# Node update of a graph network: the 35 tiles behind attention in 7 batches of 5 in place of 5 batches of 7

## The chip, the cores and the metric

One core of one Trainium2 chip runs the whole kernel. The metric is the device time of one execution in microseconds (us). Before the change it is 3775.62 us, the median of 3 runs (3770.89 to 3781.33).

## What is computed

The kernel is one attention layer and four graph convolutions over a graph of 6250 nodes with 128 features and 200000 edges. The change touches the part between them, which is done for every node alone once attention has summed its messages:

```python
agg = jax.ops.segment_sum(ft_s * a[:, :, None], dst, num_segments=n)   # 10 heads of 13
out = jax.nn.elu(agg)
out = out.reshape(n, H * DH) @ hr_w + hr_b
out = out + h_skip                       # the normalized input
out = _layer_norm(out, in_w, in_b)
skip2 = out
out = jax.nn.elu(out @ w1 + b1)          # 128 -> 512
out = jax.nn.elu(out @ w2 + b2)          # 512 -> 128
return out + skip2
...
x = x + _L0_gnn_ref(...)
h = jnp.maximum(_layernorm(x, axis=-1), 0.0)   # input of the convolutions
```

All of it is in fp32.

## The kernel before

The 6250 nodes are 49 tiles of 128 nodes. The program is a row of stages with a barrier of all engines between them: `prelude`, `attention`, `node_update`, `general_attention`, `node_update` once more (`redo`), `convolutions`. `general_attention` and the second update are behind a flag that is set only for irregular graphs; they have no rows in the trace. `attention` itself updates the first 14 tiles (FT = 2 * 7) while it runs. `node_update` takes the other 35, in MANY = 5 batches of BATCH = 7 tiles (BW = 896 nodes).

A batch i goes through these steps, with the names of the functions in the code:

- `divide` (DVE) divides the sums by the softmax denominators, `exp_attention` (ACT) and `elu_attention` (DVE) form the first ELU.
- `turn_attention` (PE) transposes the tiles into `el_ps`, `attention_turned` (ACT) copies them to `elT` and `el3T`.
- `project` (PE) is for each tile three matmuls into `el_ps`: the normalized input `hnT` against the identity, `elT` against `hr_w`, and `el3T` (the last columns and the bias) against `hr_3`. The `hnT` of the batch is loaded from DRAM into one of two buffers.
- `first_stats`, `coefficients` (DVE), `deviation`, `normal` (ACT), `second_norm` (DVE) are the layer norm; the result is `s2`, and x takes it up as well.
- `turn_second` (PE), `second_turned` (ACT copy to `s2T`).
- `quarter` 0 to 3 (PE) is the product with w1, one 128-wide part of the 512 each; `exp_quarter` (ACT) and `elu_quarter` (DVE) are its ELU, to `uT`.
- `down` (PE), in two halves a, is the product with w2; `exp_out` (ACT) and `elu_out` (DVE) give `vT`; `turn_out` (PE) transposes it back; `add_feed_forward` (DVE) adds it to x.
- `stats`, `coefficients`, `deviation`, `rectified`, `turn_h`, `hT_out` are the next layer norm and its transpose to `hT`.

The order of the work on each engine is written out by hand as a software pipeline. In cycle i PE does the transposes and quarters of batch i, the projection of batch i + 1 and the tail of batch i - 1. Two places decide what can run beside what:

```python
for i in range(-1, MANY + 1):            # PE
    if there(i):
        turn_second(i)
    if there(i + 1):
        turn_attention(i + 1)
    if there(i - 1):
        turn_out(i - 1)
    if there(i):
        quarter(i, 0)
        quarter(i, 1)
    if there(i + 1):
        project(i + 1, range(0, 2))
```

after which come quarters 2 and 3, `project` of the other tiles, `down(i, 0)`, `turn_h(i - 1)` and `down(i, 1)`. On SP's queue `once` issues the first two `hnT` loads (`first_hn`, L1862), then waits for `dis_made`, the degree factors, which DVE makes behind the layer norm of batch 0. Then `factors` stores them to `dis_tab` one fp32 value at a time (L1875), waits for that store, and issues the load of `dis_row`, the same 6272 values for all 128 partitions (L1877). Only then `later_hn` (L1867) issues the loads of batches 2 and on.

A full cycle starts where `turn_second(i)` starts. T0 to T4 are these starts of the five batches; the stage's first instruction stands at 2118.2 us of the span and its last copy to `hT` ends at 2294.0.

Of the kernel before, what the change touches and what calls it, by code (L numbers as in the profile page):

```python
# [5 lines left out]
F32 = mybir.dt.float32  # L6
# [78 lines left out]
FB = 2  # L85
FT = FB * BATCH
# [2 lines left out]
STARTS = (0, 5, 15, 20)  # L89
PHASES = 17  # L90
FINAL_AT = 130
REST_AT = 174
CQ = ((0, 393), (393, 392), (785, 392), (1177, 392))


def gnn_program(nc, t):
    out = t["out"]
# [17 lines left out]
    with top:  # L115
        def sb(name, shape, dt, on=top):
            return on.enter_context(nc.sbuf_tensor(name, shape, dt))
# [24 lines left out]
        def ln_batch(nm, on):
            return dict(st=sb(nm + "_st", [P, BATCH, 6], F32, on), mv=sb(nm + "_mv", [P, BATCH, 2], F32, on),
                        sd=sb(nm + "_sd", [P, BATCH], F32, on), rs=sb(nm + "_rs", [P, BATCH], F32, on),
                        nb=sb(nm + "_nb", [P, BATCH], F32, on))
# [13 lines left out]
        R3 = HD + 1 - P  # L159
# [26 lines left out]
        g["slot_idx"] = sb("slot_idx", [P, SPARSE, SLOTS], I32)  # L186
        g["more_idx"] = sb("more_idx", [P, SB], I32)
        g["more"] = sb("more", [P, SPARSE], F32)
        node_update(nc, t, sb, pb, sem, g, ln_batch, FB, NB, False)
        stage_over()  # L190
        general_attention(nc, t, sb, pb, sem, g)
        stage_over()
        node_update(nc, t, sb, pb, sem, g, ln_batch, 0, NB, True)
        stage_over()
        convolutions(nc, t, sb, pb, sem, g)

# [1585 lines left out]
                        nc.tensor.matmul(sum_ps[:, 0:W], oh[:], terms[:], start=True, stop=True).then_inc(s["sum_ps"], 1)  # L1782


def node_update(nc, t, sb, pb, sem, g, ln_batch, first, end, redo):

    raw, hnT_dram, x_sb, ident, eps, hT = (g[k] for k in ("raw", "hnT_dram", "x_sb", "ident", "eps", "hT"))
    hr_w, hr_3, in_w, in_b, w1, b1, w2, b2 = (g[k] for k in ("hr_w", "hr_3", "in_w", "in_b", "w1", "b1", "w2", "b2"))
# [2 lines left out]
    hs_tab, src_pad, last_deg, slot_start, slot_idx, more_idx, more = (g[k] for k in (  # L1791
        "hs_tab", "src_pad", "last_deg", "slot_start", "slot_idx", "more_idx", "more"))
    irregular, irr_part, ones, agg_tab, hT_tab = (g[k] for k in ("irregular", "irr_part", "ones", "agg_tab", "hT_tab"))
    BH = BW // 2
    R3 = HD + 1 - P
    RA = BATCH * R3
    MANY = end - first
    nm = "re_" if redo else "nu_"
    with ExitStack() as c:
        la, lb = ln_batch(nm + "ua", c), ln_batch(nm + "ub", c)  # L1800
        ex = sb(nm + "ex", [P, BATCH, HD], F32, c)
        z = sb(nm + "z", [P, BATCH, H], F32, c)
        el = sb(nm + "el", [P, BATCH, P], F32, c)
        el3 = sb(nm + "el3", [P, BATCH, R3], F32, c)
        elT = sb(nm + "elT", [P, BATCH, P], F32, c)
        el3T = sb(nm + "el3T", [RA, P], F32, c)
        hnT = [sb(nm + f"hnT{u}", [D, BATCH, P], F32, c) for u in range(2)]
        o = sb(nm + "o", [P, BATCH, D], F32, c)
        s2 = sb(nm + "s2", [P, BATCH, D], F32, c)
        s2T = sb(nm + "s2T", [D, BATCH, P], F32, c)  # L1810
        exF = [sb(nm + f"exF{u}", [P, BW], F32, c) for u in range(2)]
        uT = sb(nm + "uT", [P, 4, BW], F32, c)
        exV = sb(nm + "exV", [P, BW], F32, c)
        vT = sb(nm + "vT", [D, BW], F32, c)
        h = sb(nm + "h", [P, BATCH, D], F32, c)
# [285 lines left out]
        def _(act):  # L2101
# [94 lines left out]
        def _(pe):  # L2196

            def turn(ps, src):
                for b in range(BATCH):
# [66 lines left out]
            with wanted(pe):  # L2266
                for i in range(-1, MANY + 1):
# [566 lines left out]
```

## Time and profile before

| | |
|---|---|
| median of 3 runs | 3775.62 us |
| the profiled execution | 3790.5 us |
| its span | 3788.6 us |
| mean granted TensorE clock | 0.892 of 2.4 GHz |
| PE busy over the span | 3354.5 us (89%) |
| DVE busy | 2355.1 us (62%) |
| ACT busy | 1776.8 us (47%) |
| POOL busy | 2445.6 us (65%) |
| the stage of the change | 2118.2 to 2294.0 us |

The profile is one execution; its times are from the start of the span. A granted clock of 1.00 is TensorE at 2.4 GHz, 0.50 at 1.2 GHz. In a timeline each row is a run of like instructions on one engine, and the brackets say how long the engine was idle before and what released it. An instruction in fp32 on PE counts twice (x4 for two matmuls).

### The profile page before, as it was taken

How to read it: one execution, taken by the hardware profiler on the slowest of the kernel's cores; microseconds unless marked ns; L12 is line 12 of the kernel's file. 1: busy time of each engine (PE TensorE's matmuls, PEld its weight loads, DVE VectorE, ACT ScalarE, POOL GpSimd, SP SyncE). 2: the span in 40 equal slices, each digit the busy share in tenths (PEclk: the TensorE clock that was granted, in tenths of full speed). 3: DMA queues.
4: the chain of work that ended last, by engine and by line, in shares of the span. 5: the costliest groups of instructions: out<-in, count | busy, mean ns of one | idle time of the engine just before them, and what ended most of it. 6: DMA issues, size and time to landing. Idle time of an engine off the chain costs nothing. (4 is left out here: it accounts for less than half of the span.)

```text
span 3788.6 us, 59184 instructions
## 1 busy us (share of the span) xinstructions
PE 3354.5 (89%) x20346; PEld 2097.6 (55%) x20346; DVE 2355.1 (62%) x3512; ACT 1776.8 (47%) x4853; POOL 2445.6 (65%) x2604
## 2 busy tenths in 40 slices
PE   5788888888888888888888787999999999999999
PEld 4566666666666666666655554444544454445444
DVE  8788888888888888888865574222422242224223
ACT  4788888888888878787744353000200020002000
POOL 2577777777777777777777001777277737764775
PEclk7688888888888888888887798999999999999999
DMA  7443334333333333334332415888688868877886
GB/s 207 125 108 103 107 104 107 104 107 104 107 104 107 104 107 104 107 104 124 103 85 60 62 51 169 254 254 256 215 255 254 253 215 254 256 248 229 259 264 192
DMA packets 491674, 599.98 MB, mean 158 GB/s; under 512 B 61546, under 2 KB 422613, under 8 KB 491103
## 3 DMA queue, kind: packets, MB, share of 16 engines
q1 hardware_dynamic: 355798, 337.71, 29.3%
q0 software_dynamic: 82960, 172.57, 18.4%
q10 hardware_dynamic: 52632, 86.13, 6.3%
q8 instruction: 152, 2.49, 0.3%
q14 instruction: 132, 1.07, 0.1%
HBM read 488.79 MB, written 109.00 MB: 158 GB/s over the span
## 5 line engine op out<-in xcount | busy, mean ns | idle before, releaser
L1001 POOL DMA_INDIRECT fts<-ft_tab,src_all x1568 | 1481.2, 945 | 477.7 <-issue 477.1
L2702 PE MATMUL cv_acc<-cv_cnt,cv_parts 128*128 128x512 bf16 x3960 | 864.0, 379 | 0.0
L2453 POOL DMA_INDIRECT cv_slots<-hs_tab,slot_idx x640 | 604.8, 945 | 195.1 <-issue 195.1
L1033 DVE TENSOR_TENSOR ohk<-iota_ps,key_cols 128x784 bf16<-128x784 f32 x704 | 651.1, 966 | 5.5
L2702 PEld LDWEIGHTS cv_acc<-cv_cnt,cv_parts 128*128 128x128 bf16 x3960 | 387.2, 98 | 464.6
L1457 PE MATMUL agg_ps<-terms,oh 128*64 128x141 f32 x2744 | 557.1, 378 | 75.6 <-DVE terms L1070 75.3
L1457 PEld LDWEIGHTS agg_ps<-terms,oh 128*64 128x64 f32 x2744 | 483.2, 189 | 116.3 <-DVE terms L1070 105.4
L1218 ACT ACTIVATE dist_l<-lo_iota,low 128x128 bf16<-128x128 f16 x1760 | 533.1, 387 | 16.5 <-ACT low L1213 0.4
L1397 PE MATMUL adj_ps<-ohk,ohl 128*128 128x196 bf16 x2816 | 378.2, 261 | 89.5 <-ACT strip L1270 46.8
L1270 ACT CAST strip<-adj_ps 128x392 bf16<-128x392 f32 x704 | 334.0, 474 | 239.5 <-PE adj_ps L1400 200.4
L2702 PE MATMUL cv_acc<-raw,cv_parts 128*128 128x512 bf16 x1920 | 420.9, 379 | 0.0
L1047 DVE TENSOR_TENSOR prod<-ftd_ps,fts 128x780 f32<-128x780 f32 (+1 forms) x392 | 271.0, 691 | 225.9 <-DMA fts<-ft_tab,src_all 198.4
L1423 PE MATMUL ftd_ps<-win,ohdT 64*128 64x130 f32 x3136 | 325.8, 334 | 77.7 <-DVE prod L1047 76.4
L2453 POOL DMA_INDIRECT spare<-hs_tab,slot_idx x320 | 302.6, 946 | 97.5 <-issue 97.5
L1397 PEld LDWEIGHTS adj_ps<-ohk,ohl 128*128 128x128 bf16 x2816 | 215.2, 100 | 221.7 <-DVE ohk L1033 109.5
L1423 PEld LDWEIGHTS ftd_ps<-win,ohdT 64*128 64x128 f32 x3136 | 244.3, 219 | 157.3 <-DVE prod L1047 90.1
L2702 PEld LDWEIGHTS cv_acc<-raw,cv_parts 128*128 128x128 bf16 x1920 | 187.7, 98 | 226.7
L2669 ACT ACTIVATE cv_sd<-cv_mv,eps 128x1 f32<-128x1 f32 x2 | 0.6, 294 | 662.0 <-DVE cv_tmp L2620 662.0
L2514 DVE TENSOR_REDUCE spare<-cv_slots 128x128 f32<-128x1152 f32 x50 | 106.5, 2130 | 303.0 <-DMA cv_slots<-hs_tab,slot_idx 302.9
L1070 DVE TENSOR_TENSOR terms<-fts,most_ps 128x1040 f32<-128x1040 f32 x196 | 240.9, 1229 | 21.5 <-ACT most_ps L1249 21.2
L1083 DVE TENSOR_REDUCE score<-prod 128x80 f32<-128x1040 f32 x196 | 242.4, 1237 | 6.7
L1225 ACT ACTIVATE ohl<-dist_l 128x1280 bf16<-128x1280 bf16 x176 | 223.5, 1270 | 16.3 <-ACT dist_l L1218 0.4
(350 smaller groups left out, 3592.1 us busy)
## 6 DMA issues: line engine op xcount, KB each, us to landing
cv_cnt<-adj SPq DMA_DIRECT2D x44, 2176.0 KB
cv_cnt<-adj SPq DMA_DIRECT2D x44, 2048.0 KB
raw<-adj SPq DMA_DIRECT2D x44, 2048.0 KB
adj<-strip ACTq DMA_DIRECT2D x176, 392.0 KB
fts<-ft_tab,src_all POOLq DMA_INDIRECT x1568
win<-ft_tab SPq DMA_DIRECT2D x196, 65.0 KB
hs_tab<-cv_hs ACTq DMA_DIRECT2D x24, 448.0 KB, 3.5
cv_slots<-hs_tab,slot_idx POOLq DMA_INDIRECT x640
```

The lines of the kernel that those rows point to most:

```text
L1001: nc.gpsimd.indirect_dma_start(fts[u][:, k, :], None, ft_tab[:, :], bass.IndirectOffsetOnAxis(src_all[:, n, k:k + 1], 0)).then_inc(gathere ...
L1033: nc.vector.tensor_tensor(ohk[:, k.s, at, :], key_no.unsqueeze(1).to_broadcast([P, QC, KEYS]), columns(key_cols, k)[:, at].unsqueeze(2).to ...
L1047: nc.vector.tensor_tensor(by_half(prod[:]), ftd_ps[:, :, 0:n * HD].rearrange("p a (c f) -> p a c f", f=HD), by_half(fts[k.f][:]), ALU.mult ...
L1070: nc.vector.tensor_tensor(terms[:, k.s, :, 0:HD].rearrange("p c (h d) -> p c h d", d=DH), fts[k.f][:].rearrange("p c (h d) -> p c h d", d=DH),
L1083: nc.vector.tensor_reduce(score[:, k.c, 0:GC * H], prod[:].rearrange("p c (h d) -> p (c h) d", d=DH), AX.X, ALU.add).then_inc(score_done, 1)
L1218: last = nc.scalar.activation(dist_l[:, n, :], lo_iota[:], ACT.Abs, bias=low[:, k.s, n:n + 1], scale=-1.0)
L1270: nc.scalar.copy(strip[:, k.s, :, QS * q:QS * (q + 1), :].rearrange("p t a d -> p a t d"), adj_ps[q % 2][:, 0:QS * KEYS].rearrange("p (a t ...
L1397: nc.tensor.matmul(counts_ps[:, a * KEYS:(a + 1) * KEYS], ohl[:, k.s, n, :], ohk[:, k.s, n, :], start=(a == 0 and m == 0), stop=False)
L1423: last = nc.tensor.matmul(ftd_ps[:, half, m * HD:(m + 1) * HD], ohdT[at, k.u, (c0 + m) * P:(c0 + m + 1) * P], win[at, k.u, :], start=True, ...
L1457: nc.tensor.matmul(agg_ps[0:WD, 0:WA], oh[:, k.o, col, half, :], terms[:, k.s, n, :], start=(n == 0), stop=False)
L2453: nc.gpsimd.indirect_dma_start(slots[n % RING][:, e, :], None, hs_tab[:, :], bass.IndirectOffsetOnAxis(rows_at, 0)).then_inc(slots_in[n % ...
L2702: last = nc.tensor.matmul(a[:, 0:width], parts[:, r, b, :], cnt[q][:, 0:width // SUB, (b - b0) * SUB:(b - b0 + 1) * SUB], start=(b == 0 an ...
```

## The change

`node_update` gets the number of the first tile and the size of a batch in place of the first and last batch. The stage behind attention passes 14 and NODE_BATCH = 5, so that the same 35 tiles are MANY = 7 batches of 5; the flagged update stays with batches of 7. All tiles of SBUF that a batch uses become 5 wide, the halves of the products 320 columns in place of 448 (BH), the second part of a copy 128 columns in place of 384 (REST), and `el3T` 15 rows in place of 21 (RA). The order of the steps is the same.

```diff
+NODE_BATCH = 5
...
-        node_update(nc, t, sb, pb, sem, g, ln_batch, FB, NB, False)
+        node_update(nc, t, sb, pb, sem, g, ln_batch, FT, NODE_BATCH, False)
...
-        node_update(nc, t, sb, pb, sem, g, ln_batch, 0, NB, True)
+        node_update(nc, t, sb, pb, sem, g, ln_batch, 0, BATCH, True)
...
-def node_update(nc, t, sb, pb, sem, g, ln_batch, first, end, redo):
+def node_update(nc, t, sb, pb, sem, g, ln_batch, first, size, redo):
...
-    BH = BW // 2
+    wide_n = size * P
+    BH = wide_n // 2
+    REST = (size - 4) * P
     R3 = HD + 1 - P
-    RA = BATCH * R3
-    MANY = end - first
+    RA = size * R3
+    MANY = (NT - first) // size
...
-        hnT = [sb(nm + f"hnT{u}", [D, BATCH, P], F32, c) for u in range(2)]
+        hnT = [sb(nm + f"hnT{u}", [D, size, P], F32, c) for u in range(2)]
...
-        tiles = lambda i: slice((first + i) * BATCH, (first + i + 1) * BATCH)
-        nodes = lambda i: slice((first + i) * BW, (first + i + 1) * BW)
+        tiles = lambda i: slice(first + i * size, first + (i + 1) * size)
+        nodes = lambda i: slice(tiles(i).start * P, tiles(i).stop * P)
...
-                return nc.scalar.copy(out[:, 4:7, :].rearrange("f b p -> f (b p)"), ps[:, 1, 0:384])
+                return nc.scalar.copy(out[:, 4:size, :].rearrange("f b p -> f (b p)"), ps[:, 1, 0:REST])
...
-                for b in range(BATCH):
+                for b in range(size):
                     last = nc.scalar.activation(o[:, b, :], block_of(el_ps, b), ACT.Identity, bias=la["nb"][:, b:b + 1],
...
-                    last = nc.tensor.matmul(at, el3T[:], hr_3[:, b, :], start=False, stop=True)
-                if b == BATCH - 1:
+                    last = nc.tensor.matmul(at, el3T[:], hr_3[0:RA, b, :], start=False, stop=True)
+                if b == size - 1:
...
                     if there(i + 1):
-                        project(i + 1, range(2, BATCH))
+                        project(i + 1, range(2, size))
```

On PE, cycle 1 before begins so: the transposes of `nu_s` (its buffer s2) and `nu_el`, the transposes back, quarters 0 and 1, the first tile of `project(2)`.

```order
L2200 MATMUL nu_odd_ps<-ident,nu_s 128x128 x7
L2200 MATMUL nu_el_ps<-ident,nu_el 128x128 x7
L2217 MATMUL nu_el_ps<-ident,nu_el 21x128
L2200 MATMUL nu_back_ps<-ident,nu_vT 128x128 x7
L2240 MATMUL nu_even_ps<-nu_s2T,spare 128x448 x2
L2240 MATMUL nu_odd_ps<-nu_s2T,spare 128x448 x2
L2224 MATMUL nu_el_ps<-ident,nu_hnT 128x128
L2225 MATMUL nu_el_ps<-spare,nu_elT 128x128
L2226 MATMUL nu_el_ps<-spare,nu_el3T 128x128
```

The same place in the changed kernel:

```order
L2203 MATMUL nu_odd_ps<-ident,nu_s 128x128 x5
L2203 MATMUL nu_el_ps<-ident,nu_el 128x128 x5
L2220 MATMUL nu_el_ps<-ident,nu_el 15x128
L2203 MATMUL nu_back_ps<-ident,nu_vT 128x128 x5
L2243 MATMUL nu_even_ps<-nu_s2T,spare 128x320 x2
L2243 MATMUL nu_odd_ps<-nu_s2T,spare 128x320 x2
L2227 MATMUL nu_el_ps<-ident,nu_hnT 128x128
L2228 MATMUL nu_el_ps<-spare,nu_elT 128x128
L2229 MATMUL nu_el_ps<-spare,nu_el3T 128x128
```

Each group is five tiles and the products are 320 columns wide; nothing changes places. The first row that reads `nu_hnT` is now due after less work.

On SP's queue, from the stage's first load on, before:

```order
L1862 DMA nu_hnT<-hnT_dram 128x896 x2
L1870 DMA raw<-agg_tab 128x4x141
L1894 DMA hT<-hT_tab 128x1792
L1875 DMA dis_tab<-dis_col 128x49x1
L1877 DMA dis_row<-dis_tab 128x6272
L1867 DMA nu_hnT<-hnT_dram 128x896 x3
L1899 DMA cv_W<-in_L_gnn_W 128x128 x4
```

and in the changed kernel:

```order
L1865 DMA nu_hnT<-hnT_dram 128x640 x2
L1873 DMA raw<-agg_tab 128x4x141
L1897 DMA hT<-hT_tab 128x1792
L1878 DMA dis_tab<-dis_col 128x49x1
L1880 DMA dis_row<-dis_tab 128x6272
L1870 DMA nu_hnT<-hnT_dram 128x640 x5
L1902 DMA cv_W<-in_L_gnn_W 128x128 x4
```

The late `hnT` loads are five in place of three, 640 columns each, and stand as before behind the store of `dis_tab` and the load of `dis_row`, which are the same.

## Rows read from the trace of the kernel before

**Rows 1.** Windows of the stage: busy time of each engine, granted clock, DMA.
```profile
2118.00:2148.00 30.00, 18.32 (x65) 14.63 (x66) 15.15 (x52) 7.35 (x15) 0.86 (x4) 0.50 0.23 78
...
2173.00:2202.00 29.00, 23.54 (x108) 14.91 (x106) 21.48 (x54) 16.86 (x31) 0.00 (x0) 1.00 0.45 160
2202.00:2230.00 28.00, 24.24 (x102) 15.03 (x100) 20.85 (x54) 16.77 (x32) 0.00 (x0) 0.94 0.22 72
...
2255.00:2294.00 39.00, 21.60 (x67) 11.90 (x67) 20.37 (x55) 19.09 (x32) 0.00 (x0) 0.80 0.00 0
```

**Rows 2.** Timeline of PE: start, duration, engine, line, work, idle before and its releaser.
```profile
2126.44 0.80 PE L2224 MATMUL nu_el_ps<-ident,nu_hnT 128*128 128x128 f32 x2 [1.20 <-ACT nu_el3T L2121]
...
2138.83 0.79 PE L2226 MATMUL nu_el_ps<-spare,nu_el3T 21*128 21x128 f32 x2
...
2147.48 1.76 PE L2200 MATMUL nu_odd_ps<-ident,nu_s 128*128 128x128 f32 x7 [5.21 <-DVE nu_s L2011]
...
2172.78 0.99 PE L2200 MATMUL nu_odd_ps<-ident,nu_s 128*128 128x128 f32 x7 [1.63 <-DVE nu_s L2011]
...
2177.53 0.98 PE L2200 MATMUL nu_back_ps<-ident,nu_vT 128*128 128x128 f32 x7 [2.89 <-DVE nu_vT L1975]
...
2183.23 0.46 PE L2224 MATMUL nu_el_ps<-ident,nu_hnT 128*128 128x128 f32 x2 [1.71 <-DMA nu_hnT<-hnT_dram]
...
2188.42 0.38 PE L2224 MATMUL nu_el_ps<-ident,nu_hnT 128*128 128x128 f32 x2
...
2193.59 3.27 PE L2247 MATMUL nu_even_ps<-nu_uT,spare 128*128 128x448 f32 x8
...
2201.50 0.98 PE L2200 MATMUL nu_odd_ps<-ident,nu_s 128*128 128x128 f32 x7 [0.87 <-DVE nu_s L2011]
...
2207.23 3.19 PE L2240 MATMUL nu_even_ps<-nu_s2T,spare 128*128 128x448 f32 x4
...
2255.25 0.98 PE L2200 MATMUL nu_odd_ps<-ident,nu_s 128*128 128x128 f32 x7 [0.86 <-DVE nu_s L2011]
```

**Rows 3.** Timeline of SP, which issues loads and stores, same stage.
```profile
2148.95 0.37 SPq L1875 DMA_DIRECT2D dis_tab<-dis_col  x1
2170.78 0.32 SPq L1877 DMA_DIRECT2D dis_row<-dis_tab  x1
2171.14 22.87 SPq L1867 DMA_DIRECT2D nu_hnT<-hnT_dram  x3
```

**Rows 4.** Window of the two transfers that follow the factor store.
```profile
2171.00:2183.40 12.40, 6.17 (x32) 3.94 (x32) 11.05 (x26) 6.61 (x10) 0.00 (x0) 1.00 0.81 330
```

**Rows 5.** Timeline of DVE in the same stage.
```profile
2148.47 0.46 DVE L2039 RECIPROCAL dis_col<-nu_root 128x49 f32<-128x49 f32 x1
...
2193.70 1.49 DVE L1981 BATCH_NORM_STATS2 nu_ua_st<-nu_el_ps 128x6 f32<-128x128 f32 x7 [1.70 <-PE nu_el_ps L2226]
2195.22 0.58 DVE L1984 BATCH_NORM_AGGREGATE nu_ua_mv<-nu_ua_st 128x2 f32<-128x6 f32 x7
...
2205.05 1.15 DVE L1975 SCALAR_TENSOR_TENSOR nu_vT<-nu_even_ps,spare,nu_exV 128x896 f32<-128x896 f32 x1
```

**Rows 6.** Costliest groups by line: DVE's two additions of unequal width.
```profile
L2002 DVE TENSOR_TENSOR x_sb<-x_sb,nu_back_ps 128x512 f32<-128x512 f32 x5 | 3.4, 687 | 6.4 <-PE nu_back_ps L2200 6.4
...
L2004 DVE TENSOR_TENSOR x_sb<-x_sb,nu_back_ps 128x384 f32<-128x384 f32 x5 | 2.7, 547 | 0.0
```

**Rows 7.** Timeline of ACT in the same stage.
```profile
2196.65 2.55 ACT L2143 ACTIVATE nu_o<-nu_el_ps,nu_ua_nb,nu_ua_rs 128x128 f32<-128x128 f32 x7 [0.52 <-DVE nu_ua_nb L1991]
...
2200.07 1.28 ACT L2132 ACT_TABLE_LOAD   x1
2201.36 1.01 ACT L2132 ACTIVATE nu_exV<-nu_even_ps,spare 128x896 f32<-128x896 f32 x1
...
2293.02 0.58 ACT L2158 COPY hT<-nu_back_ps 128x512 f32<-128x512 f32 x1 [1.85 <-PE nu_back_ps L2200]
2293.51 0.48 ACT L2159 COPY hT<-nu_back_ps 128x384 f32<-128x384 f32 x1
```

More of the change, by code:

```diff
@@ L140, in gnn_program, with ln_batch @@
         dis_col = sb("dis_col", [P, NT], F32)
[L142 to L145, printed above, removed]
+        def ln_batch(nm, on, n=BATCH):
+            return dict(st=sb(nm + "_st", [P, n, 6], F32, on), mv=sb(nm + "_mv", [P, n, 2], F32, on),
+                        sd=sb(nm + "_sd", [P, n], F32, on), rs=sb(nm + "_rs", [P, n], F32, on),
+                        nb=sb(nm + "_nb", [P, n], F32, on))
         spare = sb("spare", [P, 3, BATCH * HD], F32)
@@ L1793, in node_update @@
     irregular, irr_part, ones, agg_tab, hT_tab = (g[k] for k in ("irregular", "irr_part", "ones", "agg_tab", "hT_tab"))
-    BH = BW // 2
+    wide_n = size * P
+    BH = wide_n // 2
+    REST = (size - 4) * P
     R3 = HD + 1 - P
-    RA = BATCH * R3
-    MANY = end - first
+    RA = size * R3
+    MANY = (NT - first) // size
     nm = "re_" if redo else "nu_"
     with ExitStack() as c:
[L1800 to L1805, printed above, removed]
-        el3T = sb(nm + "el3T", [RA, P], F32, c)
-        hnT = [sb(nm + f"hnT{u}", [D, BATCH, P], F32, c) for u in range(2)]
[L1808 to L1815, printed above, removed]
+        la, lb = ln_batch(nm + "ua", c, size), ln_batch(nm + "ub", c, size)
+        ex = sb(nm + "ex", [P, size, HD], F32, c)
+        z = sb(nm + "z", [P, size, H], F32, c)
+        el = sb(nm + "el", [P, size, P], F32, c)
+        el3 = sb(nm + "el3", [P, size, R3], F32, c)
+        elT = sb(nm + "elT", [P, size, P], F32, c)
+        el3T = sb(nm + "el3T", [RA, P], F32, c)
+        hnT = [sb(nm + f"hnT{u}", [D, size, P], F32, c) for u in range(2)]
+        o = sb(nm + "o", [P, size, D], F32, c)
+        s2 = sb(nm + "s2", [P, size, D], F32, c)
+        s2T = sb(nm + "s2T", [D, size, P], F32, c)
+        exF = [sb(nm + f"exF{u}", [P, wide_n], F32, c) for u in range(2)]
+        uT = sb(nm + "uT", [P, 4, wide_n], F32, c)
+        exV = sb(nm + "exV", [P, wide_n], F32, c)
+        vT = sb(nm + "vT", [D, wide_n], F32, c)
+        h = sb(nm + "h", [P, size, D], F32, c)
         el_ps = pb(nm + "el_ps", [P, 2, 512], F32, c)
@@ L1841, in node_update @@
         block = c.enter_context(nc.Block())
-        wide = [P, BATCH, D]
+        wide = [P, size, D]
         flat = lambda a: a[:].rearrange("p b d -> p (b d)")
@@ L1951, in divide @@
                 link(nc.vector.reciprocal(z[:], z[:]))
-                nc.vector.tensor_tensor(by_head, by_head, z[:].unsqueeze(3).to_broadcast([P, BATCH, H, DH]), ALU.mult
+                nc.vector.tensor_tensor(by_head, by_head, z[:].unsqueeze(3).to_broadcast([P, size, H, DH]), ALU.mult
                                         ).then_inc(s["divided"], 1)
@@ L1978, in stats @@
             def stats(ln, row):
-                for b in range(BATCH):
+                for b in range(size):
                     last = nc.vector.bn_stats(ln["st"][:, b, :], row(b))
                 link(last)
-                for b in range(BATCH):
+                for b in range(size):
                     last = nc.vector.bn_aggr(ln["mv"][:, b, :], ln["st"][:, b, :])
@@ L2003, in add_feed_forward @@
                                         back_ps[:, 0, :].rearrange("p (b d) -> p b d", d=D), ALU.add)
-                link(nc.vector.tensor_tensor(x(i)[:, 4:7, :], x(i)[:, 4:7, :],
-                                             back_ps[:, 1, 0:384].rearrange("p (b d) -> p b d", d=D), ALU.add))
+                link(nc.vector.tensor_tensor(x(i)[:, 4:size, :], x(i)[:, 4:size, :],
+                                             back_ps[:, 1, 0:REST].rearrange("p (b d) -> p b d", d=D), ALU.add))
             def second_norm(i):
@@ L2141, in normal @@
                 wait(act, s["s2"], i)
-                for b in range(BATCH):
+                for b in range(size):
                     last = nc.scalar.activation(o[:, b, :], block_of(el_ps, b), ACT.Identity, bias=la["nb"][:, b:b + 1],
@@ L2149, in rectified @@
                 wait(act, s["h_turned"], i)
-                for b in range(BATCH):
+                for b in range(size):
                     last = nc.scalar.activation(h[:, b, :], x(i)[:, b, :], ACT.Relu, bias=lb["nb"][:, b:b + 1],
@@ L2158, in hT_out @@
                 nc.scalar.copy(hT[:, at:at + 512], back_ps[:, 0, :])
-                nc.scalar.copy(hT[:, at + 512:at + BW], back_ps[:, 1, 0:384]).then_inc(s["hT"], 1)
+                nc.scalar.copy(hT[:, at + 512:at + wide_n], back_ps[:, 1, 0:REST]).then_inc(s["hT"], 1)
             def factor_roots():
@@ L2198, in turn @@
             def turn(ps, src):
-                for b in range(BATCH):
+                for b in range(size):
                     last = nc.tensor.transpose(ps[:, b // 4, (b % 4) * P:(b % 4 + 1) * P], src(b), ident[:])
```

## The prediction

> **What bounds the kernel now.** I read the page first: PE is busy 89% of the span. The stage of the change is 175.8 us of it, 2118.2 to 2294.0, under 5%. Then windows over the stage [rows 1]: no engine is full there, PE has 18.3 us of the first 30 at a granted clock of 0.50 (1.2 GHz), 23.5 of 29 and 24.2 of 28 in two full cycles, and 21.6 of the last 39. So the chain from engine to engine decides, and I read it in the timelines. The starts of `turn_second` on PE [rows 2] cut it: T0 2147.5, T1 2172.8, T2 2201.5, T4 2255.3; the stage ends at 2294.0. The pieces are start 29.3, cycle 0 25.3, cycle 1 28.7, cycles 2 and 3 53.8, last batch with its tail 38.7: 175.8. Within a full cycle PE waits twice for a chain through the other engines: before `turn_second` (0.87 before T2) and before `turn_out` (2.89 in cycle 1). The third wait is 1.71 for the load of `hnT` of batch 2, at 2183.2 [rows 2]. The SP queue tells why [rows 3]: the factor store is issued at 2148.95, the load of `dis_row` at 2170.78, when the store has landed, and `hnT` right behind it. The window from 2171.0 to 2183.4 moved 330 GB/s [rows 4], 4.1 MB: `dis_row` (3.2 MB) and two `hnT` (0.46 MB each). So this `hnT` is ready 34.3 us after the store is issued.
>
> **How long a piece takes at five tiles.** DVE: `dis_col`, from which the store follows, is made at 2148.47; statistics are 1.48 us for seven tiles; the last step of vT takes 1.15 [rows 5]. Two additions of 512 and 384 columns take 0.687 and 0.547 [rows 6], 1.1 ns a column: 256 columns fewer save 0.27 of an operation 896 wide. (In-place min and add run at about twice that rate, from the starts of their neighbours; I take 0.13.) ACT: copies of 512 and 384 columns take 0.58 and 0.48, 0.8 ns a column, so 0.2 is saved; the layer norm's seven activations take 2.55, 0.36 each; a table load is 1.28, whatever the batch, and exV is 1.01 [rows 7]. PE at full clock: `down` is 3.27 for eight instructions 448 wide, so five sevenths; five tiles of projection take 5.17 (2188.42 to 2193.59), 1.03 each; at half clock 1.88 each (2126.44 to 2139.6, seven tiles) [rows 2]. The work for a tile costs the same, so PE's sum for 35 tiles is nearly kept. What the change can win is filling and draining; what it repeats is the fixed cost of a cycle.
>
> **The start, −7.3.** All of it is one chain: the four wide operations ahead of the first transpose (−1.0), two transposes fewer at half clock (−0.4), copies (−0.2), two tiles of projection at half clock (−3.8), statistics and their sums (−0.6), normal (2 × 0.36 = −0.7), two wide operations on DVE (−0.5). T0 is 2140.2. `dis_col` moves with it.
>
> **Cycle 0, 19.5 in place of 25.3.** No `turn_out` is in it. Saved: four transposes (−0.8), quarters and down (two sevenths of 12.4 = −3.5), two tiles (−2.1), together −6.4 where all at full clock; the wait before T1 stays, and since T0 comes at half clock, a slightly larger share of the shorter cycle lies there: +0.6. T1 is 2159.7.
>
> **A full cycle, 20.1.** From T: DVE adds x (0.8) and divides (1.5), vT is ready at T+3.7 and `turn_out` starts (4.75 before, 2172.78 to 2177.53); transposes to 4.4; quarters 0 and 1 to 6.6; two tiles of projection to 8.7; quarters 2 and 3 to 10.9; three tiles to 14.0. uT of quarter 3 is ready at 13.4, so `down` need not wait. From the end of projection, T2 came 7.9 us later before (2193.59 to 2201.50): statistics 2.1, normal 2.55, two wide operations 2.2, links 1.0. At five tiles that is 6.1, so 20.1; PE's own work in it is 5.0, so its wait grows from 0.87 to 1.1. Cycle 1 without its wait for the load is 27.0, and 27.0 × 5/7 would be 19.3: the part that does not shrink costs 0.8 in each cycle.
> The table load lies ahead of exV in each cycle: there are two a batch, so four more. I cost it at nothing, since DVE is busy with x and division until T+2.3 and exV is ready at T+1.2; without that cover each would put up to 1.28 us on `turn_out`.
> The Trainium skill, ScalarE: Activation LUTs, section "Table sets: the hidden batching unit", has the rule that speaks against this change: do all exps together, then all roots, since each switch of set loads a table, for which it gives about 2.7 us. The trace has 1.28. By the page's figure exV is ready at T+2.6, 0.3 behind DVE, and the sum would be about 2 us more.
>
> **The new wait: cycle 1, 31.1.** The store is issued 7.5 us earlier, at 2141.4, with DVE's start. It takes the same 21.8 to the next issue, for its 6272 values are the same, and the transfers behind it move 3.9 MB in place of 4.1: 11.4 us. `hnT` of batch 2 is there at 2174.6. The first projection of it comes due at T1+6.6 = 2166.3. That is the core of the prediction: cycle 0 shrinks by 5.8 and the piece ahead of the projection by 3.8 or so, but the store and `dis_row` do not shrink at all. PE waits 8.3 where it waited 1.7. PE is in order, so quarters 2 and 3, `down` and the chain to T2 stand behind it; SP's later loads are not late. After an idle time like this the clock should be at half: it was at 0.50 from the start of the stage, behind such a gap [rows 1], and `quarter` 0 of cycle 2 took 3.19 for four instructions, as long as `down` takes for eight, behind two waits of under 3 [rows 2]. Two tiles at 1.88 and a quarter at double cost 2.7 more. Bounds: nothing, if the clock holds; 6, if it is low to the end of the projection. Cycle 1 is 20.1 + 8.3 + 2.7 = 31.1, T2 2190.8.
> By the Trainium skill, TensorE: Matmul & The Clock Gate, "HAM oscillation", a wait for a DMA between bursts drops the clock for the next burst. That is the row's side too; the sum is the same by both.
>
> **The rest.** Cycles 2 to 4: 60.3. Cycle 5 has no division ahead of it: 19.0. Clock drops: cycle 2 before lost 1.5 so (0.94 in its window), one of three; five sevenths of that at one in three in four cycles is 1.4. The last batch with its tail: 38.7 before, with the clock at 0.80. Its chain saves two sevenths of nine PE pieces and DVE's and ACT's wide operations: −9.0, to 29.7. The end is 2190.8 + 60.3 + 19.0 + 1.4 + 29.7 = 2301.2, which is **+7.2** on 2294.0. The stage after starts from the same barrier and gets no other data. Other fixed costs (11 more matmul waits, more instruction words) lie beside these chains.
> Against the profiled execution that is 3790.5 + 7.2 = 3797.7. It stands 14.9 above the median of the runs; I carry the difference over: 3775.6 + 7.2 = **3782.8**. About 0.3%, 11.3 us, is what a measurement of this kernel can tell from no change; the three runs spread over 10.4.
>
> **Rivals.**
> *Low clock in every cycle (slower).* Place: `turn_out` and quarter 0 of cycles 2 to 6. PE there works 1.4 between waits of 1.1 and 2.3, less than before. If each cycle pays 1.5 to 2.2 in place of 1.4 in all, that is +7.6: the end is +14.8, 3790. It decides from three more drops of 1.4 on (past +11.3). For: 3.19 in cycle 2, 0.80 in the tail. Against: cycle 1 had waits of 1.63 and 2.89 as well and kept 1.00.
> *Load in time (even, or faster).* If the store lands sooner, or `hnT` passes `dis_row`, 8.3 and 2.7 fall out: −3.8, 3771.8. For: nothing ties the store to PE. Against: PE resumed at 2183.23, just when the traffic behind the store ended.
> *Table loads on the path (slower).* By the rule above, as a mechanism here: if DVE did not cover them, four more loads of 1.28 are 5.1: +12.3, 3787.9. The trace bears little of it: in cycle 2 exV was ready at 2202.4 and vT's last step began only at 2205.05, its first 0.65 earlier.
> *No change at all*, if the flagged update were the one that runs: it has no rows, so 1 in 50.
>
> **How the numbers follow.** Forecast 0.62, of which 0.07 past 11.3 by measurement or a longer low clock; low clock 0.12; table loads 0.03; load in time 0.16, of which 0.02 past −11.3; no change 0.02; something that wins over 11.3: 0.02; something unseen within: 0.03. Faster 0.04, slower 0.22, same 0.74. The range goes from the load in time with 2 off, 3770, to the low clock, 3790.5.
>
> **What would show it.** `hnT` of batch 2 as releaser of a PE wait of 7 to 10 us near 2175; PEclk near 0.5 right behind it; seven starts of `turn_second`, the full ones 20 to 21 apart; T0 near 2140; the tail near 30. I am wrong if that wait is under 3, if full cycles are over 21.5, or if the convolutions' span moves.

## The result and the profile after

The changed kernel takes 3789.73 us (median of 6 runs, 3788.11 to 3799.52), the kernel before in the same comparison 3776.44 (6 runs). The ratio is 1.0040, 95% interval 1.0026 to 1.0055: slower by 0.4%, 13.3 us between the medians. (The ratios in this text are estimated from all fast runs; they can lie some 0.1% off the quotient of the two medians, which is 1.0035 here.)

The spans of the two profiled executions do not show it: 3788.6 before, 3787.7 after. The execution profiled before reached the stage at 2118.2, the one after at 2104.5, 13.7 us earlier, through attention, which the change does not touch. That is the spread of single executions: in all the kernels profiled here the stage starts between 2098.3 and 2118.2. From the end of the stage to the end of the span it is 1494.6 us before and 1493.5 after, so the convolutions did not move. The stage itself grew from 175.8 us to 189.7, by 13.9, and this is the number to explain.

Windows of the stage after, cut at the starts of `turn_second`; columns are busy us of PE, its weight loads, DVE, ACT and POOL, the granted clock, DMA share and GB/s:

```profile
2104.00:2126.00 22.00, 13.63 (x48) 10.82 (x48) 11.33 (x47) 6.01 (x13) 0.86 (x4) 0.50 0.28 94
2126.00:2145.00 19.00, 17.28 (x73) 12.66 (x73) 13.39 (x36) 11.35 (x19) 5.08 (x5) 0.88 1.12 7
2145.00:2180.00 35.00, 23.87 (x83) 16.61 (x83) 17.06 (x46) 13.65 (x28) 0.00 (x0) 0.71 0.34 122
2180.00:2200.00 20.00, 16.72 (x83) 12.12 (x83) 16.15 (x45) 13.39 (x28) 0.00 (x0) 1.00 0.06 17
2200.00:2223.00 23.00, 19.27 (x84) 14.02 (x85) 16.83 (x47) 13.95 (x28) 0.00 (x0) 0.85 0.11 27
2223.00:2244.00 21.00, 17.97 (x83) 13.19 (x83) 15.87 (x45) 13.02 (x28) 0.00 (x0) 0.92 0.34 104
2244.00:2265.00 21.00, 18.23 (x84) 13.42 (x85) 14.31 (x41) 13.53 (x27) 0.00 (x0) 0.92 0.00 0
2265.00:2294.00 29.00, 15.21 (x57) 9.65 (x57) 15.97 (x46) 15.25 (x28) 0.00 (x0) 0.83 0.00 1
```

Against [rows 1]: the start is shorter, at the same 0.50. Cycle 0 is shorter too. Then there is one window of 35 us, at 0.71, and of the five that follow only one is at 1.00. PE is busy for 142 of 190 us in place of 134 of 176: the work is nearly the same, and more of it ran at 1.2 GHz (granted clock over the stage 0.81 in place of 0.85).

Timeline of PE after, at T0, T1, in cycle 1, at T2, in cycle 3 and at T6:

```profile
2126.62 1.33 PE L2203 MATMUL nu_odd_ps<-ident,nu_s 128*128 128x128 f32 x5 [3.45 <-DVE nu_s L2014]
...
2145.47 0.77 PE L2203 MATMUL nu_odd_ps<-ident,nu_s 128*128 128x128 f32 x5 [1.57 <-DVE nu_s L2014]
...
2149.14 1.33 PE L2203 MATMUL nu_back_ps<-ident,nu_vT 128*128 128x128 f32 x5 [2.24 <-DVE nu_vT L1978]
...
2152.39 2.27 PE L2243 MATMUL nu_odd_ps<-nu_s2T,spare 128*128 128x320 f32 x4
2162.09 0.77 PE L2227 MATMUL nu_el_ps<-ident,nu_hnT 128*128 128x128 f32 x2 [7.42 <-DMA nu_hnT<-hnT_dram]
...
2168.10 2.34 PE L2243 MATMUL nu_odd_ps<-nu_s2T,spare 128*128 128x320 f32 x4
...
2172.83 0.49 PE L2227 MATMUL nu_el_ps<-ident,nu_hnT 128*128 128x128 f32 x2
...
2180.03 0.76 PE L2203 MATMUL nu_odd_ps<-ident,nu_s 128*128 128x128 f32 x5 [1.02 <-DVE nu_s L2014]
...
2203.90 1.33 PE L2203 MATMUL nu_back_ps<-ident,nu_vT 128*128 128x128 f32 x5 [2.25 <-DVE nu_vT L1978]
2205.03 2.34 PE L2243 MATMUL nu_even_ps<-nu_s2T,spare 128*128 128x320 f32 x4
...
2264.90 0.76 PE L2203 MATMUL nu_odd_ps<-ident,nu_s 128*128 128x128 f32 x5 [1.25 <-DVE nu_s L2014]
```

The starts and the end, from the same timeline, against the prediction:

| piece | before | forecast | after |
|---|---|---|---|
| start | 29.3 | 22.0 | 22.1 |
| cycle 0 | 25.3 | 19.5 | 18.9 |
| cycle 1 | 28.7 | 31.1 | 34.6 |
| cycles 2, 3, 4 | | 60.3 + 1.4 (to cycle 5) | 20.2, 22.7, 21.6 |
| cycle 5 | | 19.0 | 20.4 |
| last batch and tail | 38.7 | 29.7 | 29.3 |
| stage | 175.8 | 183.0 | 189.7 |

SP's queue after:

```profile
2127.83 0.37 SPq L1878 DMA_DIRECT2D dis_tab<-dis_col  x1
2149.94 0.32 SPq L1880 DMA_DIRECT2D dis_row<-dis_tab  x1
2150.30 66.64 SPq L1870 DMA_DIRECT2D nu_hnT<-hnT_dram  x5
```

The order is that of [rows 3]: the store is issued when batch 0 is through its norm, 22.1 us go by to the load of `dis_row`, and `hnT` of batch 2 releases PE 12.2 us after that, at 2162.09. PE had waited 7.42, and 1.71 before.

Two things are lost, then: the wait that was forecast, and TensorE's clock, in more places than were forecast. In cycle 1 `turn_out` and both quarters ahead of the wait already run at half speed (2.27 for a quarter that takes 1.24), and behind the wait the clock is low until 2171. In cycle 3 it falls at `turn_out` again (1.33 in place of 0.76 us, then 2.34 for quarter 0). Each time it is the place where PE has waited for s2 (1.57 in cycle 1, 1.24 in cycle 3) and then 2.25 for vT. The place alone does not decide: in cycle 2 the waits were 1.02 and 2.25, and the clock stayed up.

### The profile page after: what moved, and what is told of

Read it like the earlier page. It is cut to its first block and busy times, and to the rows that moved or that the text cites. A ratio compares the mean times of both kernels' runs of the same rounds, so it can differ in the third digit from the quotient of the medians.

```text
span 3787.7 us, 59458 instructions
## 1 busy us (share of the span) xinstructions
PE 3352.7 (89%) x20412; PEld 2108.3 (56%) x20412; DVE 2364.6 (62%) x3562; ACT 1787.6 (47%) x4887; POOL 2446.5 (65%) x2604
## 3 DMA queue, kind: packets, MB, share of 16 engines
q1 hardware_dynamic: 356086, 337.71, 29.3%
## 5 line engine op out<-in xcount | busy, mean ns | idle before, releaser
L1071 DVE TENSOR_TENSOR terms<-fts,most_ps 128x1040 f32<-128x1040 f32 x196 | 240.9, 1229 | 21.6 <-ACT most_ps L1250 21.2
```

The costliest lines, as they stand in the source:

```text
L1071: nc.vector.tensor_tensor(terms[:, k.s, :, 0:HD].rearrange("p c (h d) -> p c h d", d=DH), fts[k.f][:].rearrange("p c (h d) -> p c h d", d=DH),
```

## Experiments

All stages and cycles below are from the timelines of each run, one execution each, as above. Expectations take 190.4 for the stage after, from a first reading; the end of the last copy, 2294.2, makes it 189.7. Medians are of separate comparisons with the kernel before. Its median was 3776.4 beside the change, 3774.6 beside `e5_hn_first`, `e7_hn_first`, `e5_busy` and `e5_no_tables`, 3781.2 beside `e5_hn_first_busy_short`, `e7_store_twice` and the two `busy_pre`, and 3775.0 beside the other four. Two executions of the same work differ as well: cycle 0 is 18.9 or 19.4 in kernels that are alike up to there, and the last batch is 29.5 and 28.3 in `e5_busy_short` and `e5_hn_first_busy_short`, which have the same code for it. So single differences of about 1 us in this table carry no weight.

| run | cycles 0, 1, 2, ... | start | last and tail | stage | median | ratio to before |
|---|---|---|---|---|---|---|
| before | 25.3, 28.7, 28.5, 25.3 | 29.3 | 38.7 | 175.8 | | |
| after | 18.9, 34.6, 20.2, 22.7, 21.6, 20.4 | 22.1 | 29.3 | 189.7 | 3789.7 | 1.0040 |
| e5_hn_first | 19.4, 23.0, 21.8, 22.8, 21.7, 20.5 | 22.1 | 29.4 | 180.6 | 3778.2 | 1.0002 (0.9991 to 1.0014) |
| e7_hn_first | 25.3, 27.2, 27.2, 25.3 | 29.3 | 38.4 | 172.7 | 3774.4 | 0.9997 (0.9986 to 1.0008) |
| e5_busy | 18.9, 35.3, 21.5, 21.5, 21.5, 19.7 | 22.1 | 29.7 | 190.1 | 3791.8 | 1.0038 (1.0021 to 1.0056) |
| e5_no_tables | 18.9, 35.0, 21.8, 21.7, 22.8, 18.6 | 22.1 | 28.8 | 189.5 | 3793.5 | 1.0042 (1.0029 to 1.0055) |
| e5_busy_short | 19.4, 33.3, 20.2, 20.2, 20.2, 19.0 | 22.1 | 29.5 | 183.9 | 3786.7 | 1.0023 (1.0009 to 1.0038) |
| e5_hn_first_busy_short | 18.9, 20.2, 20.2, 20.2, 20.2, 19.1 | 22.1 | 28.3 | 169.3 | 3771.3 | 0.9982 (0.9966 to 0.9997) |
| e7_hn_first_busy_short | 25.3, 27.2, 27.2, 25.4 | 29.3 | 39.0 | 173.4 | 3774.0 | 0.9994 (0.9980 to 1.0007) |
| e7_store_twice | 25.3, 57.5, 29.8, 25.3 | 29.3 | 36.1 | 203.3 | 3804.7 | 1.0068 (1.0044 to 1.0092) |
| e5_hn_first_busy_pre | 18.9, 20.2, 20.2, 20.2, 20.2, 19.1 | 19.6 | 28.3 | 166.7 | 3764.4 | 0.9968 (0.9951 to 0.9985) |
| e7_hn_first_busy_pre | 25.3, 27.2, 27.2, 25.4 | 22.7 | 37.7 | 165.5 | 3766.8 | 0.9962 (0.9947 to 0.9976) |
| e5_all_waits | 17.7, 20.2, 20.2, 20.2, 20.2, 19.0 | 19.5 | 27.7 | 164.8 | 3761.5 | 0.9970 (0.9956 to 0.9985) |
| e7_all_waits | 23.7, 27.2, 27.2, 25.4 | 23.9 | 35.3 | 162.7 | 3761.6 | 0.9972 (0.9954 to 0.9989) |

### The load of batch 2 ahead of the store

```diff
+            sp.wait_ge(s["projected"], 1)
+            sp.dma_start(hnT[0][:].rearrange("f b p -> f (b p)"), hnT_dram[:, nodes(2)]).then_inc(hn_in[0], 16)
             sp.wait_ge(s["dis_made"], 1)
             factors(sp)
-            later_hn(sp)
+            later_hn(sp, 1)
```

`later_hn(sp, 1)` starts at batch 3. With batches of 5:

> Batches of 5; only the hnT load of batch 2 is moved ahead of the factor store on SP's queue (its buffer is free once batch 0 is projected, some 7 us before the factors are made). Theory A (the wait for this load, and the half clock behind it, are most of the loss): PE's wait of 7.4 us for hnT is gone, cycle 1 falls from 34.6 to between 20.1 and 22.7, the stage from 190.4 to 176 to 179 us, and the median from 3789.7 to 3776 to 3779. Rival B (the clock falls in every cycle because PE works too little between its waits, whatever the load does): cycle 1 loses only the wait itself, 7 us, stage 183 or more.

With batches of 7, the kernel before:

> Batches of 7 with the same move of the load. Both theories: PE's wait of 1.7 us for hnT of batch 2 goes, cycle 1 falls from 28.7 to 27.0, the stage from 175.8 to about 174; the median moves by less than its spread. If more than 3 us come back, the load of dis_row disturbs more than this wait.

SP's queue with batches of 5 has the load (L1899) 7.3 us ahead of the store:

```profile
2130.53 0.32 SPq L1899 DMA_DIRECT2D nu_hnT<-hnT_dram  x1
2137.81 0.37 SPq L1878 DMA_DIRECT2D dis_tab<-dis_col  x1
2160.99 0.32 SPq L1880 DMA_DIRECT2D dis_row<-dis_tab  x1
```

PE has no wait for `hnT` any more, and the stage is 180.6, 9.1 shorter: more than the wait of 7.4 alone, less than theory A wanted. It is still 4.8 longer than with batches of 7 before. Windows of cycles 1 to 3 of this run, and `turn_out` and quarter 0 of cycle 1 on PE:

```profile
2156.00:2179.00 23.00, 19.52 (x83) 14.12 (x83) 16.48 (x46) 13.08 (x27) 0.00 (x0) 0.85 0.47 170
2179.00:2200.80 21.80, 18.30 (x84) 13.42 (x84) 16.44 (x46) 13.63 (x28) 0.00 (x0) 0.92 0.05 15
2200.80:2223.60 22.80, 19.32 (x83) 13.92 (x83) 16.49 (x46) 13.58 (x28) 0.00 (x0) 0.85 0.11 27
```

```profile
2159.65 1.32 PE L2205 MATMUL nu_back_ps<-ident,nu_vT 128*128 128x128 f32 x5 [2.25 <-DVE nu_vT L1980]
2160.78 2.34 PE L2245 MATMUL nu_even_ps<-nu_s2T,spare 128*128 128x320 f32 x4
```

The granted clock is 0.85, 0.92, 0.85, and a cycle is 23.0, 21.8, 22.8 with it. So the clock falls without any load being late. Neither theory stands alone: the load is the greater part, and rival B, the low clock in every cycle, is true beside it. With batches of 7 the same edit gives back 3.1 us: 1.5 in cycle 1, and 1.3 in cycle 2, whose clock drop did not come in this execution; whether the moved load prevented it is not shown. Its full cycles are at 1.00.

### Idle work for PE in the waits

```diff
+            def busy(ps, n):
+                for _ in range(n):
+                    nc.tensor.matmul(ps[:, 0, 0:256], ident[:], w1[:, 0:256], start=True, stop=True)
+
             def turn_second(i):
-                pe.wait_ge(s["s2"], i + 1)
                 wait(pe, s["uT"], 4 * i)
+                if not redo and i:
+                    busy(odd_ps, 4)
+                pe.wait_ge(s["s2"], i + 1)
...
             def turn_out(i):
-                pe.wait_ge(s["v"], i + 1)
                 wait(pe, s["hT"], i)
+                if not redo:
+                    busy(back_ps, 8 if i < MANY - 3 or i == MANY - 2 else 4)
+                pe.wait_ge(s["v"], i + 1)
```

> Batches of 5 with PE given idle work: 8 (4 in the cycle before last) matmuls of 256 columns that nobody reads, into the empty back_ps ahead of the wait for v, and 4 into the empty odd_ps ahead of the wait for s2, in every cycle; the load order is as in the change. They fill 1.8 of the 2.25 us and 0.9 of the 1.25 us of wait at full clock. Theory B: with the waits filled the clock stays at 2.4 GHz in cycles 2 to 6, cycles 3, 4 and 5 fall from 22.7, 21.6 and 20.4 to 20.2, 20.2 and 19.0, and the stage from 190.4 to 184 to 186, with the wait of 7 to 9 us for hnT still there. Theory A alone (no price for the clock but behind the load): cycles 3 to 5 stay and the stage stays at 190 or gets longer, since the fillers only delay PE.

These matmuls, the fillers, write to a part of PSUM that is empty at that moment. The stage stayed at 190.1, so by its number theory A alone would seem right. The cycles say otherwise. Two pairs of rows of PE in this run, idle work (L2208) and the transposes behind it:

```profile
2183.32 3.62 PE L2208 MATMUL nu_back_ps<-spare,ident 128*128 128x256 f32 x16
2186.77 0.71 PE L2203 MATMUL nu_back_ps<-ident,nu_vT 128*128 128x128 f32 x5
...
2201.86 1.89 PE L2208 MATMUL nu_odd_ps<-spare,ident 128*128 128x256 f32 x8
2203.58 0.71 PE L2203 MATMUL nu_odd_ps<-ident,nu_s 128*128 128x128 f32 x5
```

The clock is 1.00 in cycles 2 to 5, but eight fillers take 3.4 us and not 1.8, since each fp32 matmul is two instructions of 0.22: they ran over the waits, and each cycle is 21.5, 1.3 too long. The size was my mistake. With 4 (2 in the later cycles) and 2, still without moving the load:

> Batches of 5 with the short idle work (4 and 2) alone; the load of batch 2 stands where it stood in the change. It separates the two causes: stage 169.3 (both mended) plus the wait for hnT (7.4 to 9.4) plus the half clock behind it (2 to 4), so 179 to 183; full cycles 20.2 at a granted clock of 1.00.

The stage is 183.9, 5.8 below the change and 0.9 above the expected range; the full cycles behind cycle 1 are 20.2 each. PE in cycle 1 of this run:

```profile
2155.06 0.76 PE L2203 MATMUL nu_back_ps<-ident,nu_vT 128*128 128x128 f32 x5 [0.51 <-DVE nu_vT L1978]
...
2167.80 0.76 PE L2235 MATMUL nu_el_ps<-ident,nu_hnT 128*128 128x128 f32 x2 [9.82 <-DMA nu_hnT<-hnT_dram]
...
2171.52 2.50 PE L2251 MATMUL nu_even_ps<-nu_s2T,spare 128*128 128x320 f32 x4
```

`turn_out` is at full speed now (0.76), PE reaches the projection sooner and so waits 9.82 in place of 7.42 for the same load; behind the wait two tiles and quarter 2 (2.50) are at half clock. With both edits:

> Batches of 5, the load of batch 2 moved ahead as in the first run, and idle work on PE at half the length of the run before: 4 matmuls of 256 columns ahead of the wait for v (2 in the last cycles), 2 ahead of the wait for s2. In that run a filler took 0.43 us and not 0.22, so that 8 and 4 of them were longer than the waits and made each cycle 1.3 us longer; 4 and 2 take 1.7 and 0.9. If the two causes (load wait, clock falling in the short cycles) are all that is lost, the full cycles are 20.2 at a granted clock of 1.00 and the stage is 170 to 173 us, 3 to 5 below the batches of 7 in the kernel before. If something else costs, the stage stays over 175.

Start, cycles 1 to 4 together, and last batch of that run:

```profile
2101.00:2123.10 22.10, 13.63 (x49) 10.82 (x49) 11.92 (x48) 6.03 (x13) 0.86 (x4) 0.50 0.34 109
...
2142.00:2222.90 80.90, 77.21 (x380) 57.24 (x380) 65.29 (x181) 54.00 (x108) 0.00 (x0) 1.00 0.29 88
...
2242.00:2270.30 28.30, 15.47 (x65) 10.02 (x65) 15.91 (x46) 15.60 (x28) 0.00 (x0) 0.88 0.00 0
```

The stage is 169.3, every full cycle 20.24 at 1.00. That is 20.4 below the change: 9.1 for the load and 5.8 for the idle work each by itself, and 5.5 that neither gives alone. By cycles, 1.6 of the 5.5 lie in cycle 1, where the long wait hides low clock in front of it and is followed by half clock whatever PE did before. The others lie in cycle 0 (1.0), cycles 2 to 5 (1.8) and the last batch (1.2); there the clock rose or fell at another place from one execution to the next, and what of that the edits did is not separated. The same with batches of 7 (6 and 1 fillers):

> The twin of e5_hn_first_busy_short with batches of 7: load moved, idle work of 6 and 1 in the two waits, nothing at the start. Stage 171 to 172.5 (the last batch gains up to 1.5), 2 to 3 us above the 169.3 of batches of 5: what 7 batches of 5 are worth when neither the load nor the clock stands against them.

173.4, where 171 to 172.5 were expected: the last batch won nothing there (39.0). So 7 batches of 5 are 4.1 us ahead in the stage once the load is in time and the clock is up in the full cycles, still with the start at 0.50. That is one execution each; the two ratios, 0.9982 and 0.9994, have intervals that overlap.

### The store twice

```diff
                 sp.dma_start(dis_tab.rearrange("(t p) -> p t", p=P), dis_col[:]).then_inc(dis_out, 16)
+                sp.wait_ge(dis_out, 16)
+                sp.dma_start(dis_tab.rearrange("(t p) -> p t", p=P), dis_col[:]).then_inc(dis_out, 16)
-            sp.wait_ge(dis_out, 16)
+            sp.wait_ge(dis_out, 32)
```

> The kernel before with batches of 7, and the store of the factors done twice, one behind the other, with the same values. The later loads of SP come 21.8 us later. Theory A: the loss is the wait for hnT of batch 2, whatever the size of a batch. PE's wait grows from 1.7 to 23 to 24 us, and the clock is at 0.50 behind it for some 4 to 6 us, 2 to 4 us lost: the stage goes from 175.8 to between 199 and 202, the median up by 23 to 27. If the wait is partly covered by other work, it is less than 20.

SP's queue and the row of PE that waits for the load:

```profile
2129.10 0.37 SPq L1875 DMA_DIRECT2D dis_tab<-dis_col  x1
2151.60 0.37 SPq L1877 DMA_DIRECT2D dis_tab<-dis_col  x1
2175.16 0.33 SPq L1879 DMA_DIRECT2D dis_row<-dis_tab  x1
```

```profile
2187.51 0.77 PE L2226 MATMUL nu_el_ps<-ident,nu_hnT 128*128 128x128 f32 x2 [25.81 <-DMA nu_hnT<-hnT_dram]
```

The first store takes 22.5 to the next issue, the second 23.6; the wait grows by 24.1, from 1.71 to 25.81, and cycle 1 by 28.8, from 28.7 to 57.5. The other 4.7 are the half clock behind the wait: two tiles and two quarters (0.77 for the first row of a tile, as in the change). The stage grows by 27.5, since cycle 2 was 1.3 longer and the last batch 2.6 shorter, both with the granted clock (0.89 for 0.94, 0.88 for 0.80). A wait for this load is paid in full with batches of 7 too. The change did not make the load dearer (22.1 for the store in place of 21.8); it made it due earlier.

### Table loads

This kernel leaves out the square root, so that ACT need not switch tables for it.

```diff
-                nc.scalar.activation(ln["sd"][:], ln["mv"][:, :, 1], ACT.Sqrt, bias=eps[:]).then_inc(sd, 1)
+                nc.scalar.activation(ln["sd"][:], ln["mv"][:, :, 1], ACT.Identity, bias=eps[:]).then_inc(sd, 1)
```

> Batches of 5; in the two layer norms of the update ACT forms var + eps (Identity) in place of its square root, so that 14 of the 15 table loads of ACT go and the output of the norms is scaled wrongly, same shapes and traffic. If DVE covers the loads, as the prediction has it, the full cycles 2 to 4 stay within 0.3 us of 20.2 at equal clock and only the last batch's tail can lose up to 1.3 us: stage 188 to 190. If the loads are on the path to turn_out, each full cycle is 1.3 shorter: stage near 183.

Windows of cycles 2 to 4:

```profile
2181.60:2203.30 21.70, 18.30 (x83) 13.17 (x83) 16.39 (x45) 11.03 (x25) 0.00 (x0) 0.92 0.06 15
2203.30:2225.00 21.70, 18.24 (x83) 13.36 (x83) 16.37 (x46) 11.04 (x25) 0.00 (x0) 0.92 0.12 28
2225.00:2247.80 22.80, 19.34 (x84) 13.99 (x84) 16.48 (x46) 11.03 (x25) 0.00 (x0) 0.85 0.31 96
```

ACT is busy 11.0 in a cycle in place of 13 to 14. At a clock of 0.92 a cycle is 21.7, as in cycle 4 of the change (21.6), at 0.85 it is 22.8 (22.7 in its cycle 3). So the loads of a full cycle are covered, as costed. (The stage has 17 of them, 15 went; the expectation miscounted.) Cycle 5, without a division, is 18.6 where it is 19.0 at full clock elsewhere, and the last batch is 0.5 shorter: about 1 us in all, within what differs between executions. Taking 15 loads out of the stage was not worth more than that.

### Lifting the clock at the start, and holding it everywhere

```diff
+            if not redo:
+                for _ in range(4):
+                    nc.tensor.matmul(odd_ps[:, 0, :], ident[:], w1[:, 0:512], start=True, stop=True)
             with wanted(pe):
```

> As e5_hn_first_busy_short, with 4 idle matmuls of 512 columns on PE at the start of the stage, while DVE and ACT form the first ELU. The clock is at half through the whole start (22.1 us) of every run so far. If the work ahead of it lifts the clock to 2.4 GHz, the projection of batch 0 takes 5.2 in place of 9.4 us and the start 16 to 18; if the clock stays at 0.50 there, the start stays at 22.1 and only 0 to 1 us changes.

> The same three edits on batches of 7 (6 and 1 idle matmuls in the two waits, 4 of 512 columns at the start). Its full cycles lost nothing to the clock in the run with the load alone (27.2 at 1.00), so the idle work can win only in the last batch (38.4, clock 0.80) and at the start: 2 to 4 us in the one, 5 to 6 in the other if the clock rises. Stage 172.7 to between 163 and 170. If batches of 5 are better once their two costs are gone, this one stays 2 to 4 us above its twin with 5.

Windows of the run with batches of 7: the idle work, the first transposes and projection, the wait ahead of T0, and the first work behind T0:

```profile
2109.60:2114.60 5.00, 4.97 (x8) 2.08 (x8) 3.72 (x8) 0.96 (x1) 0.86 (x4) 0.67 0.80 243
2114.60:2124.40 9.80, 8.60 (x52) 6.57 (x51) 4.55 (x24) 3.54 (x6) 0.00 (x0) 1.00 0.30 116
2125.90:2132.30 6.40, 0.01 (x1) 0.01 (x1) 4.92 (x16) 2.85 (x8) 0.00 (x0) 0.55 0.16 62
2132.30:2137.00 4.70, 4.70 (x18) 3.97 (x19) 3.72 (x10) 2.16 (x6) 2.13 (x2) 0.53 0.30 2
```

The projection of batch 0, which ran at 0.50 in every other kernel [rows 1, 2], runs at 1.00. Starts are 22.7 for 7 tiles and 19.6 for 5; with 5 the idle work stayed at half speed for longer and ended 2.4 us behind the first ELU, so 2.5 us were won in place of 4 to 6. With that, batches of 7 are 1.2 shorter (165.5 against 166.7), where they were expected 2 to 4 longer. The clock fell in the idle stretch ahead of T0 in both. The last two kernels fill that wait (13 or 9 fillers) and the four of the last batch:

> e5_hn_first_busy_pre with idle work also in the wait ahead of T0 (9 matmuls of 256 columns, wait 4.7) and in the four waits of the last batch and tail (2, 5, 4, 11). The clock, which fell in the wait before T0, stays up in cycle 0 (18.9 to about 17.9), and in the tail (28.3 to 27). Stage 166.7 to about 164.5.

> The same with batches of 7 (13 in the wait of 6.4 ahead of T0; 2, 6, 6, 14 behind). Cycle 0 from 25.3 to about 23.5, the last batch with its tail from 37.7 to 34 to 35. Stage 165.5 to 160 to 162. Then batches of 7 are the shorter ones once the clock is held everywhere; if batches of 5 are, it is by their shorter start and tail.

Start, full cycles, last batch with batches of 7, then the same with 5:

```profile
2099.30:2123.20 23.90, 21.98 (x97) 15.34 (x97) 14.64 (x52) 7.36 (x15) 0.85 (x4) 0.88 0.35 118
...
2146.90:2226.70 79.80, 77.53 (x346) 50.61 (x346) 60.11 (x154) 50.07 (x93) 0.00 (x0) 1.00 0.24 83
2226.70:2262.00 35.30, 30.91 (x129) 20.87 (x129) 20.00 (x54) 18.84 (x31) 0.00 (x0) 1.00 0.00 0
```

```profile
2100.20:2119.70 19.50, 17.82 (x75) 11.91 (x75) 11.92 (x48) 6.01 (x13) 0.86 (x4) 0.86 0.37 124
...
2137.40:2237.30 99.90, 95.70 (x471) 70.84 (x471) 79.06 (x220) 66.89 (x134) 0.00 (x0) 1.00 0.23 71
2237.30:2265.00 27.70, 23.58 (x105) 17.15 (x105) 15.97 (x46) 15.60 (x28) 0.00 (x0) 1.00 0.00 1
```

The clock is at 1.00 from T0 on, and 0.88 and 0.86 in the starts. The stages are 162.7 and 164.8 (expected 160 to 162, and about 164.5), and batches of 7 are the shorter ones, by 2.1. About 1.0 of that is the idle work at the start, which ran 2.3 us past the first ELU with batches of 5 and 1.3 with batches of 7. Both kernels are faster than the one before, by 0.28% and 0.30% with intervals that overlap almost wholly: which of the two is the better one is not settled by their medians (3761.6 and 3761.5), only by the stage.

## Why the prediction was wrong

It forecast +7.2 and gave 74% to a change too small to measure; it is +13.3 by the medians, +13.9 in the stage. The start (22.0, measured 22.1), cycle 0 (19.5, 18.9), the full cycle at full clock (20.1, measured 20.2), the last batch (29.7, 29.3), table loads at nothing, and the new wait for `hnT` of batch 2 with its cause on SP's queue all held. `e7_store_twice` and `e5_hn_first` show that cause by making the wait and by taking it away.

The step that failed is the term "Clock drops" in "The rest": 1.4 us in four cycles, from one drop in three cycles before. Cycles 2 to 5 took 84.9 where 79.3 were forecast at full clock: 5.6 in place of 1.4. I priced a drop by how often it came with batches of 7. In the runs with batches of 5 it nearly always comes: behind the waits of 1.25 for s2 and of 1.1 to 2.25 for vT, with only 1.4 of work between them, it fell in cycles 1, 3, 4 and 5 of the change, and in all of cycles 1 to 5 of `e5_hn_first`. With the waits filled it fell in none of these cycles. So the waits are shown to be the cause; why batches of 7, with waits of 1.63 and 2.89 in cycle 1, kept the clock there is not shown. The rival "Low clock in every cycle" had the place and the mechanism right, and got 0.12. That its +14.8 came near was luck in part: it had 9.0 for the drops of five cycles, and cycles 2 to 5 lost 5.6, with nothing beyond the forecast in the last batch; cycle 1 made up the rest.

The second miss is the sum for cycle 1, 34.6 for 31.1, and half of it is the price of the half clock behind the wait. It held through two tiles, both quarters and part of the next tile, where two tiles and one quarter were taken: from the projection to T2 it is 17.9, for 13.8 at full clock (cycle 2). So it cost 4.1 for the 2.7 taken, within the bound of 6; the same piece at full clock was forecast at 13.5, 0.3 too low. The load of `hnT` landed 16.6 behind T1 in place of 14.9. Of these 1.7, 0.65 is cycle 0, which was that much shorter than forecast, 0.3 the store, and 0.75 the transfers behind it: 12.15 for 11.4, where the 330 GB/s of [rows 4] would make 11.7 of 3.9 MB. Together 3.4. The wait itself, 7.42, came out below the 8.3 forecast only because PE reached it late, at half clock; with the idle work ahead of it, in `e5_busy_short`, it is 9.82.

What the change was to win also holds for one clock only, which the prediction did not say. With both losses mended it is 4.1 (169.3 against 173.4). With the clock lifted in the start and held from T0 on, batches of 7 are ahead by 2.1 in the stage. Of the 6.2 between, 2.8 are in the start (29.3 and 22.1, then 23.9 and 19.5) and 3.1 in the last batch and its tail (39.0 and 28.3, then 35.3 and 27.7): filling and draining a batch of 7 at half clock is what the smaller batch saved. It is one execution of each kernel, 1.0 is the longer overrun of the idle work, and the medians do not decide.

## What to carry to other kernels

When a batch gets smaller, list what does not shrink: a store or load of fixed length that a later load stands behind on the same queue does not get shorter, so all that the pipeline gains between its issue and the use of the later load is given back as a wait. What is gained ahead of its issue is kept, as the start here. Price TensorE's clock for each cycle from the waits of the new cycle, not from how often it fell in the old one; and where PE waits anyway, work that nobody reads can be a cheap fix, if it is measured to be shorter than the wait. A comparison of two batch sizes holds only for the clock it was made at.

## What the runs showed of the hardware that was not expected

TensorE was busy nearly without a gap for 13 us of fp32 projections of 128 columns and stayed at 0.50 (2126.44 to 2139.6, [rows 2]). Behind four matmuls of 512 columns the same projections ran at 1.00 (window 2114.6 to 2124.4 above). The same work, then, did not lift the clock in one kernel and did not let it fall in the other.

The store of 6272 single fp32 values, 24.5 KB, took 20.7 to 26.6 us from its issue to the next in all the kernels profiled here, more than the 3.2 MB of `dis_row` behind it, which with two `hnT` took 12.
